# Two tables of sorted rows, pad rows written behind the first layer's gathers, and three later loads, in a two-layer graph and mixture-of-experts kernel

## What is computed

```python
xn = _layernorm(x)
x = x + gnn0(xn, src, dst, edge_weight) + mix0(xn)
# layer 0's experts: each row goes to ONE of 8
probs = softmax(H @ Wg + bg); assign = argmax(probs)
x = x + probs[assign] * (H @ Wd[assign] + bd[assign])      # H = gelu(norm(x) @ W1 + b1)
xn = _layernorm(x)
x = x + gnn1(xn, src, dst) + mix1(xn)
# layer 1's experts: each row goes to TWO of 8
_, idx = top_k(norm(x) @ Wg + bg, 2)
x = x + sum_over_two(gelu(norm(x) @ W1[e] + b1[e]) @ W2[e] + b2[e])
```

## Time and profile before

| what | value |
|---|---|
| median of 3 runs | 3153.93 us (3152.07 to 3159.39) |
| the profiled execution's own time | 3154.51 us |
| its span, first to last instruction | 3152.9 us |
| granted PE clock, mean | 0.869 of 2.4 GHz |
| PE busy | 2439.5 us, 77% of the span |
| DVE, ACT, POOL busy | 1160.9, 1074.9 and 594.1 us |
| DMA | 202.08 MB, mean 64 GB/s |

### The profile page before, as it was taken

The page is one execution under the profiler, slowest core; times in us unless marked ns, Lnnn a source line. Parts: engine busy times, 40 slices in busy tenths (PEclk is TensorE's granted clock), DMA queues, the critical chain, the costliest instruction groups (busy, mean ns, idle before and its releaser), DMA issues.

```text
span 3152.9 us, 39103 instructions
## 1 busy us (share of the span) xinstructions
PE 2439.5 (77%) x11905; PEld 1947.2 (62%) x11906; DVE 1160.9 (37%) x2481; ACT 1074.9 (34%) x1977; POOL 594.1 (19%) x482
## 2 busy tenths in 40 slices
PE   0775899989898898965899278687878787925787
PEld 0444688868677786753788246565656565614676
DVE  4444677753545536421000423214142323320111
ACT  3222677755464555611333211111111111112222
POOL 1610011100101001021122111112221212023454
PEclk9887899998897989976899688897989897957999
DMA  3321011110101101043222341312121212053443
GB/s 119 97 71 59 31 34 44 49 52 20 63 24 51 43 23 64 22 120 89 74 68 60 110 157 54 83 36 66 45 68 43 73 38 76 7 136 67 82 83 63
DMA packets 162715, 202.08 MB, mean 64 GB/s; under 512 B 59800, under 2 KB 131119, under 8 KB 162580
## 3 DMA queue, kind: packets, MB, share of 16 engines
q0 software_dynamic: 75168, 89.11, 12.3%
q1 hardware_dynamic: 75834, 100.45, 9.6%
q10 hardware_dynamic: 11578, 10.82, 1.1%
HBM read 108.51 MB, written 93.74 MB: 64 GB/s over the span
## 4 chain that ended last, share of the span: by engine, by line
PE 51%; DMA 24%; another core or an unknown queue 12%; DVE 4%; ACT 3%; issue 3%; SPq 1%; POOL 1%; ACTq 0%; DVEq 0%; POOLq 0%
PE bank L711 47%; DMA agg_rows<-agg_t 17%; PE bank L717 4%; DMA arena<-agg_rows 3%; DMA out_rows<-arena,ids_cur 1%; POOL w_adj L563 1%; SPq L401 1%; ACT t L1115 1%; DMA xg<-expert_rows 1%; DMA arena<-in_x 1%; DMA feat<-xg 1%; ACT count_a L1154 0%; ACT w_qc L1154 0%; ACT w_adj L1153 0%
## 5 line engine op out<-in xcount | busy, mean ns | idle before, releaser
L711 PE MATMUL bank<-xg,w_adj 125*125 125x256 f32 (+1 forms) x2500 | 648.8, 397 | 0.1
L711 PEld LDWEIGHTS bank<-xg,w_adj 125*125 125x125 f32 x2500 | 453.2, 194 | 62.1 <-issue 1.2
L711 PEld LDWEIGHTS bank<-arena,row_hot 128*125 128x125 f32 x3200 | 424.7, 198 | 84.9 <-issue 64.9
L711 PE MATMUL bank<-arena,row_hot 128*125 128x100 f32 x3200 | 433.1, 282 | 43.4 <-remote 19.7
L717 PE MATMUL bank<-ident,arena 125*128 125x125 f32 (+1 forms) x650 | 147.0, 353 | 392.9 <-remote 292.2
L717 PEld LDWEIGHTS bank<-ident,arena 125*128 125x128 f32 (+1 forms) x650 | 89.8, 175 | 446.6 <-issue 441.4
L711 PE MATMUL bank<-t,w_h 128*128 128x250 f32 (+1 forms) x1184 | 328.4, 431 | 17.0 <-remote 10.8
L1153 ACT ACTIVATE w_adj<-bank 125x200 f32<-125x200 f32 x400 | 217.4, 544 | 271.8 <-PE bank L711 265.3
L1513 DVE TENSOR_TENSOR row_hot<-iota_all,arena 128x2000 f32<-128x2000 f32 x100 | 223.8, 2238 | 230.5 <-PE bank L711 227.6
L711 PEld LDWEIGHTS bank<-t,w_h 128*128 128x128 f32 x1184 | 231.7, 201 | 110.4 <-issue 58.1
L711 PE MATMUL bank<-w_adj,arena 128*125 128x256 f32 x1024 | 241.1, 393 | 0.2 <-DVEq L1798 0.2
(11 more groups left out here) (313 smaller groups left out, 2917.6 us busy)
## 6 DMA issues: line engine op xcount, KB each, us to landing
count_a<-counts POOLq DMA_DIRECT2D x25, 781.2 KB
sorted_in<-pad_rows POOLq DMA_DIRECT2D x16, 878.4 KB, 16.9
arena<-sorted_in SPq DMA_DIRECT2D x49, 251.0 KB
counts<-count_a SPq DMA_DIRECT2D x13, 781.2 KB
counts<-w_qc SPq DMA_DIRECT2D x12, 781.2 KB
arena<-rows_b SPq DMA_DIRECT2D x5, 1875.0 KB
w_adj<-in_L_ffn_Wd POOLq DMA_DIRECT2D x8, 1024.0 KB, 6.3
w_adj<-in_L_ffn_W POOLq DMA_DIRECT2D x16, 512.0 KB, 5.8
```

The source lines that it names most:

```text
L711: return pe.matmul(o, w, r, start=first, stop=last, skip_group_check=not check)
```

## The change

1. `sorted_in` becomes two tables, one for each layer. `zero_tails`, `ends`, `tail_tab`, `tails_known` and `tails_stored` go away.
2. All rows of both tables are written with pad rows during the gathers of layer 0: behind the gather of block b, `pads(b // 12, b % 12)` writes `FILL` = 2250 rows for b from 0 to 23, 24 transfers. The first scatter into a table waits until its 12 have landed.
3. The weights of experts 0 and 1 are issued only when the last step has its sums (`last_begun`); in layer 0 the scatter of the step before the last goes ahead of them.
4. The load of the residual rows moves behind the results of expert 0 of layer 0, ahead of the weights of expert 2.
5. `routes()` goes ahead of four DVE instructions at the end of layer 0.

```diff
-TAIL = G * B + PT
+FILL = E0 * CAP // B // 12 * B
...
-        sorted_in = nc.dram_tensor("sorted_in", (E0 * CAP, D + 1), F32).ap()
-        marks = nc.dram_tensor("marks", (4, D), F32).ap()
+        sorted_in = [nc.dram_tensor(f"sorted_in{n}", (E0 * CAP, D + 1), F32).ap() for n in range(2)]
+        marks = nc.dram_tensor("marks", (5, D), F32).ap()
...
-            pool.dma_start(sorted_in[0:1, :], pad_rows[0:1, :]).then_inc(scattered, 16)
+            pool.dma_start(marks[4:5, :], pad_rows[0:1, 0:D]).then_inc(scattered, 16)
...
                 for e in range(E0):
                     results_out(layer, e)
+                    if layer == 0 and e == 0:
+                        pool.wait_ge(rowx_free, 16)
+                        pool.dma_start(h_big, by_part(rows_x)).then_inc(rowx_in, 16)
                     if e + 2 < E0:
                         expert_w(layer, e + 2)
...
-            def scatter(n, src):
+            def pads(layer, n):
+
+                rows_of = sorted_in[layer][FILL * n:FILL * n + FILL, :].rearrange("(i p) d -> p i d", p=B)
+                pool.dma_start(rows_of, pad_rows[:, :].unsqueeze(1).to_broadcast([B, FILL // B, D + 1])).then_inc(
+                    pads_stored[layer], 16)
+
+            def scatter(layer, n, src):
...
-            def zero_tails(layer):
-
-                take(pool, tails_known)
-                for e in range(E0):
-                    tail = pool.value_load(tail_tab[0:1, e:e + 1], min_val=CAP * e, max_val=CAP * e + N - G * B)
-                    pool.dma_start(sorted_in[ds(tail, TAIL), :].rearrange("(i p) d -> p i d", p=B),
-                                   pad_rows[:, :].unsqueeze(1).to_broadcast([B, TAIL // B, D + 1])).then_inc(tails_stored, 16)
-                pool.wait_ge(tails_stored, 16 * E0 * (layer + 1))
...
             for b in range(NB):
                 if b >= P0 + AB and (b - P0) % AB == 0:
-                    scatter(1, y_ids)
+                    if b == P0 + AB:
+                        pool.wait_ge(pads_stored[0], 16 * 12)
+                    scatter(0, 1, y_ids)
                 gather(0, b, feat0, 0)
+                if b < 24:
+                    pads(b // 12, b % 12)
             pool.wait_ge(graph_done, 1)
+            scatter(0, 1, y_ids)
+            take(pool, last_begun)
             for e in range(2):
                 expert_w(0, e)
-            scatter(1, y_ids)
-            zero_tails(0)
-            scatter(1, y_ids)
-
-            pool.wait_ge(rowx_free, 16)
-            pool.dma_start(h_big, by_part(rows_x)).then_inc(rowx_in, 16)
+            scatter(0, 1, y_ids)
+
             expert_results(0)
...
-                    scatter(2, r_ids)
+                    if b == NQ + 1 + AP:
+                        pool.wait_ge(pads_stored[1], 16 * 12)
+                    scatter(1, 2, r_ids)
                 gather(1, b, feat1, total)
             pool.wait_ge(graph_done, 2)
+            take(pool, last_begun)
             for e in range(2):
                 expert_w(1, e)
-            zero_tails(1)
-            scatter(2, r_ids)
+            scatter(1, 2, r_ids)
             expert_results(1)
...
-                    ends()
+                    dve.sem_inc(last_begun, 1)
...
             layer0(NS - 1, 0)
+            routes()
             chain(dve.tensor_reduce(inv_out[:, :], deg_all.rearrange("p b (h c) -> p c (b h)", h=2), AX.X, ALU.add))
...
             chain(dve.reciprocal(inv_out[:, :], inv_out[:, :]))
-            routes()
             experts(0)
```

More of the change, by code:

```diff
@@ L176, in program @@
         before_tab = sb("before_tab", [1, E0], I32)
-        tail_tab = sb("tail_tab", [1, E0], I32)
         pair_tab = sb("pair_tab", [1, E0], I32)
@@ L327, in program @@
         pos_full, scattered = sem("positions_made"), sem("rows_scattered")
-        routes_full, tails_known, tails_stored, sorted_done = (
-            sem(n) for n in ("routes_made", "tails_known", "tails_stored", "results_stored"))
+        routes_full, last_begun, sorted_done = (
+            sem(n) for n in ("routes_made", "last_step_begun", "results_stored"))
+        pads_stored = [sem(f"pad_rows_stored{layer}") for layer in range(2)]
         xin_full, xin_free = sem("sorted_rows_loaded"), sem("sorted_rows_used")
@@ L393, in sorted_rows @@
                         take(sp, xin_free)
-                        sp.dma_start(x_in, pair_rows(sorted_in, e, t)).then_inc(xin_full, 16)
+                        sp.dma_start(x_in, pair_rows(sorted_in[layer], e, t)).then_inc(xin_full, 16)
                 take(sp, xin_free)
-                sp.dma_start(x_in, pair_rows(sorted_in, 0, 0)).then_inc(xin_full, 16)
+                sp.dma_start(x_in, pair_rows(sorted_in[layer], 0, 0)).then_inc(xin_full, 16)
             sp.dma_start(e_i32, a["dst"].rearrange("(q n) -> q n", q=TR)).then_inc(l_edge, 16)
@@ L660, in scatter @@
                         pool.indirect_dma_start(
-                            sorted_in, bass.IndirectOffsetOnAxis(ap=pos_cur[:, k, i:i + 1], axis=0),
+                            sorted_in[layer], bass.IndirectOffsetOnAxis(ap=pos_cur[:, k, i:i + 1], axis=0),
                             src[:, i, :], None).then_inc(scattered, 16)
-            def zero_tails(layer):
-                take(pool, tails_known)
-                for e in range(E0):
-                    tail = pool.value_load(tail_tab[0:1, e:e + 1], min_val=CAP * e, max_val=CAP * e + N - G * B)
-                    pool.dma_start(sorted_in[ds(tail, TAIL), :].rearrange("(i p) d -> p i d", p=B),
-                                   pad_rows[:, :].unsqueeze(1).to_broadcast([B, TAIL // B, D + 1])).then_inc(tails_stored, 16)
-                pool.wait_ge(tails_stored, 16 * E0 * (layer + 1))
             pool.wait_ge(tabs_ready, 1)
@@ L1772, in routes @@
                 dve.sem_inc(routes_full, 1)
[L1774 to L1778, removed]
             def experts(layer):
```

## The result

The changed kernel takes 3171.4 us (median of 6 runs, 3166.5 to 3183.1) where the kernel before takes 3151.8 (3149.2 to 3159.4): ratio 1.0065, interval 1.0046 to 1.0085, some 20 us slower. The profiled execution has a span of 3170.1 us.

What follows compares the result with a forecast made beforehand. A chain 51% PE, 24% DMA, where DMA counts only if a transfer ends a wait. Gains 23.7 + 26.5 less 15 give 35; pad writes in POOL's queue lose 50: +15 on 3154.5, 3170 us; range 3112 to 3215, forecast's own 3161 to 3215.

Steps and rivals of the forecast that it cites:

- The queue serves in order, and the edge loads wait behind the pad writes: Layer 0 gathers, POOL's queue: the next block's edge load waits behind each pad write; 50 us lost in blocks 2 to 9.
- The first rival (they hide): Layer 0 gathers: edge loads don't wait behind pad writes, or these run at 121 GB/s without drift; 3119 us, chance 0.24.
- The duration of a pad write: Layer 0 gathers: one write of 2313 KB on 125 partitions was taken to occupy POOL's queue for 26.9 us.
- the bounds given (19.1 to 42): Pad write duration in us: lower end at the residual rows' rate, far upper end scaled from the last three old pad writes.
- the same formula: Blocks 2 to 9: each later than the one before by 3.2 + 3.0 + 1.0 + 26.9 + 2.6 - 28.9 = 7.8 us.
- the third rival: Layer 0 gathers: SP's count stores share engines, pad writes take 31 us, net +48, 3202 us; within the forecast's 0.52.
- The sign that I gave: POOL's timeline: idle time from `edge_tail` to gather grows from 6.2 us to 13, then near 19.
- The slack of 12 us: Layer 0 blocks: POOL may wake at 19 us instead of 6.8 before PE lacks gathered rows; 12 us of drift free.
- Pads 9 to 23 at nothing: Layer 0 from block 10 on: row-wise work lies between blocks, so these pad writes were costed at nothing.
- Gain at the end of layer 1, 23.7: Scatter no longer waits for pad rows, 18.1 us; last sums without weights beside them, 5.6 us.
- Gain at the end of layer 0, 26.5: Sums 7.0 us shorter, first sorted rows 13.9 shorter, and PE's second wait, for the second sorted rows, of 5.64 gone.
- The moved load, 15 us: Layer 0, before expert 2: residual rows ahead of its weights on POOL's queue make PE 12 to 18 us late, 15 taken.

## Why the prediction was right

The forecast (+15, 3170) came out at +17 to +20. By its own steps:

- **The queue serves in order, and the edge loads wait behind the pad writes: right**, and shown twice over, by the same writes in SP's queue (POOL's blocks 28.9 to 29.9 us apart again) and by shorter ones. The first rival (they hide) was wrong for 125 partitions and right for 90.
- **The duration of a pad write: mis-sized, with a second error against it.** I took 26.9 us. Between the end of a write's issue and POOL's next wake pass 33 us in the mean of blocks 3 to 9 (28.9 to 37.3), so about 29 without the 1.0 and 2.6 of start and fixed part; inside the bounds given (19.1 to 42). The gather's issue I put at 3.2 us; behind a long wait it takes 1.25. By the same formula a block is then late by 1.3 + 2.8 + 33 - 28.9 = 8.2 us, and 8 x 8.2 - 12 = 54 against 50 predicted and 48.7 measured between blocks 1 and 9. That the errors of +2 and -2 us cancel within a block is luck. The source of the 26.9 us was wrong too: within a write the rate is 108 GB/s (494 to 503), not 86, and by estimate 2313 KB would take 21.4 us at it. The rest passes while other transfers are in flight (share 0.44, 74 GB/s from 485 to 488) or while few engines still work (0.10 from 470 to 473). That points to the third rival, the stores of counts on the same engines, but no run isolates it. The sign that I gave also failed in part: POOL's idle time grows to 24 to 32 us (30.76 and more above), not to near 19.
- **The slack of 12 us: about right.** Block 1's load took 12.6 us and cost 0.5; block 2's took 19.7 and cost 0.8. But the blocks don't grow evenly (38.7, 31.5, 41.7, 30.2, 33.8, 45.0 us); the sum holds, not the single one.
- **Left out: the clock.** Its mean fell from 1.00 to between 0.82 and 0.93 in blocks 3 to 8, and PE's busy time rose by 13.6 us. The sum came out right without it because POOL's queue, not PE, spaces these blocks; I hadn't worked that out. Left out too: in two of the blocks PE has the gathered rows some 10 us after the gather's start (545.25 to 555.43, 654.54 to 664.38), where I had 3.2 + 4.9. These are the two longest blocks (41.7 and 45.0 us); in the others it is some 4 to 5 us.
- **Pads 9 to 23 at nothing: right** for the time (0.9994 with them alone), though block 10 took 7 us longer behind the first.
- **Gain at the end of layer 1, 23.7: right.** The wait for the pad rows gave 17.8 (18.9 down to 1.1; 18.1 predicted), the sums 6.0 (5.6). The distance fell from 43.9 to 18.4 us, by 25.5, 1.7 more than these two. One term was wrong in the working: 627 KB at 121 GB/s are 5.3 us, not 5.6, so the sums should have been put at 7.9 us; they took 7.8.
- **Gain at the end of layer 0, 26.5: right.** Sums 5.7 (7.0), first sorted rows 14.1 (13.9), second wait 5.6: 25.4; by the distances 28.5 from block 24 to the end of expert 0. That the sums are shorter is here due to the scatters' place ahead of the weights, not to the wait, as the run with early weights showed.
- **The moved load, 15 us: too low.** It cost 19.9 us until expert 2 and 2.7 behind it, 22.6. The load takes 41.4 us to land, not the 32.8 worked out from the rate alone, and the scatters of expert 1 wait too: DVE's copy of the row numbers waits 32.3 us for them. In five pieces there is no wait, and the medians differ by 17.4 us. Where the 8.6 us between 32.8 and 41.4 go isn't shown.

Sum predicted -35 + 50; measured -31.3 + 48.5. By the Trainium skill ("DMA: Bandwidth & Descriptors", "Anatomy of one DMA") a pad write would take an estimated 7.3 us in any of the layouts; the runs show landings of 31.1, 21.4 and 13.8 us, so it is out by a factor of four for 125 partitions, of three for 50 and of two for 90. The rule of its section "Why a DMA increments its semaphore by 16 and not by 1" (the Trainium skill, "DMA: Bandwidth & Descriptors") fits the runs of 125, 90, 50 and 25 partitions, as 5, 15, 10 and 5 engines: the DMA shares within a write are 0.32, 0.93, 0.62 and 0.32.

## What to carry to other kernels

A background transfer isn't hidden because the engines are idle: ask in which queue it goes, how long it occupies it, and what small load is issued behind it. If the write and what else stands with it in the queue last longer than the spacing of the loads behind it, the queue falls behind each time; here both POOL's and SP's did. Before moving such a write, lay it out so that it is short (here 90 or 50 partitions rather than 125, same bytes, 44% or 69% of the time to land), and cut a large load that goes ahead of urgent ones into pieces with room between.

## What was not expected of the hardware

- The page counts 1200 more packets for each pad write of 125 or 25 partitions than for one of 90 (107424 against 78624 over 24 writes), and 304 more with 50; the bytes are the same within 0.5 MB.
- A queue that falls behind stops its engine: SP took up to 49.6 us to issue one load of 1250 KB, and in the old tail writes POOL stands some 31 us ahead of the sixth (31.02 us in the kernel with the pad writes alone).
- Two kernels that only write a further table in layer 0 are 7 us slower at the end of layer 1, 5.7 to 5.9 of it in the wait for the old tail writes; a third with the same table but 15 writes waits no longer than before (19.02 us). Why isn't settled.
